# The pair loop's neighbour sums on TensorE moved one slot later, between two expert layers, and the output projection moved behind a first layer

## What is computed

```
xn  = layernorm(x)
gnn = segment_sum((xn @ W[rel])[src] * edge_weight, dst)        # 16 relations, 100,000 edges
mix = (attention(xn) * sigmoid(gelu(norm(xn) @ Wg1) @ Wg2)) @ Wproj + bproj
x   = x + gnn + mix
t   = layernorm(x)                                              # statistics of the new x
rw, re = top_2(softmax(t @ router.T)); combine = scatter(rw, re)
out = x + t + sum_e combine[:, e] * (gelu(t @ w1[e] + b1[e]) @ w2[e] + b2[e])
```

## Time and profile before

| | |
|---|---|
| median of 3 runs | 1621.45 us (1619.91 to 1625.02) |
| profiled execution | 1623.3 us, its span 1621.6 us |
| busy: TensorE, VectorE, ScalarE, GpSimd | 97%, 83%, 60%, 64% of the span |
| first phase | up to about 745 us |
| iterations 2 to 23 of the pair loop | 804 to 1544 us, 33.61 us each in the mean |

### The profile page before, as it was taken

How to read it: one execution, slowest core, us unless ns; L and a number is a source line. 1 busy time by engine, 2 the same in 40 slices (tenths; PEclk the granted TensorE clock), 3 DMA queues, 4 the chain that set the end, 5 groups by cost and what they waited for, 6 DMA issues and landing times.

```text
span 1621.6 us, 31747 instructions
## 1 busy us (share of the span) xinstructions
PE 1579.1 (97%) x10509; PEld 1442.6 (89%) x10509; DVE 1346.7 (83%) x3391; ACT 965.5 (60%) x2156; POOL 1030.0 (64%) x1109
## 2 busy tenths in 40 slices
PE   6899999999999999998699999999999999999998
PEld 5788888888888888887699999999999999999998
DVE  7878665488888888874699999999999999999985
ACT  4454222255655655553677766777667777677764
POOL 3443322577777777746777777777777777777720
PEclk9999999999999999999899999999999999999999
DMA  8677665688899888878433333343333333333320
GB/s 264 204 262 259 240 259 225 214 289 281 272 287 295 273 283 285 285 249 299 143 110 117 101 100 111 105 118 99 101 112 103 117 102 102 112 104 114 105 58 10
DMA packets 127076, 290.50 MB, mean 179 GB/s; under 512 B 21271, under 2 KB 49724, under 8 KB 126914
## 3 DMA queue, kind: packets, MB, share of 16 engines
q1 hardware_dynamic: 86068, 177.19, 29.8%
q0 software_dynamic: 39952, 110.13, 25.8%
q10 hardware_dynamic: 894, 1.16, 0.2%
HBM read 149.49 MB, written 138.90 MB: 178 GB/s over the span
## 4 chain that ended last, share of the span: by engine, by line
PE 68%; DVE 18%; issue 6%; ACT 3%; POOL 3%; DMA 1%; DVEq 0%; ACTq 0%; POOLq 0%
PE bank L1767 54%; DVE ml L1552 3%; DVE xres L1682 3%; DVE ht L1668 2%; POOL raw L685 2%; PE bank L1970 2%; PE bank L1811 2%; PE bank L1812 2%; DVE sel L1536 2%; PE bank L1971 2%; PE bank L1822 1%; PE bank L1922 1%; ACT mh L1010 1%; ACT raw L1066 1%; PE bank L1966 1%
## 5 line engine op out<-in xcount | busy, mean ns | idle before, releaser
L799 POOL DMA_INDIRECT stg<-table,idxcur x495 | 560.0, 1131 | 215.8 <-issue 114.7
L1767 PE MATMUL bank<-wreg,xt 128*128 128x512 f32 x2352 | 583.3, 399 | 4.9 <-DVE wreg L1151 2.3
L1767 PEld LDWEIGHTS bank<-wreg,xt 128*128 128x128 f32 x2352 | 436.6, 190 | 94.2 <-DVE wreg L1151 2.5
L685 POOL DMA_INDIRECT raw<-table,idxa x297 | 304.6, 1026 | 87.7 <-issue 75.6
L1767 PE MATMUL bank<-tt,wreg 128*128 128x256 f32 (+1 forms) x2400 | 318.6, 282 | 2.2 <-DVE tt L1618 2.2
L1767 PE MATMUL bank<-wreg,ht 128*128 128x256 f32 x2352 | 313.1, 282 | 0.2 <-DVE ht L1668 0.2
L1767 PEld LDWEIGHTS bank<-tt,wreg 128*128 128x128 f32 x2400 | 295.8, 189 | 5.4 <-issue 2.6
L1767 PEld LDWEIGHTS bank<-wreg,ht 128*128 128x128 f32 x2352 | 291.3, 188 | 0.4 <-DVE ht L1668 0.4
L1066 ACT ACTIVATE raw<-bank,cols 128x256 f32<-128x256 f32 (+1 forms) x400 | 165.0, 464 | 96.9 <-PE bank L1767 96.9
L1193 DVE COPY stg<-bank 128x512 f32<-128x512 f32 x196 | 133.6, 686 | 97.2 <-PE bank L1767 96.5
L1552 DVE SCALAR_TENSOR_TENSOR ml<-stg,nrm,mh 128x256 fp32r<-128x256 f32 x455 | 195.7, 480 | 16.0 <-ACT mh L1010 15.7
(11 more groups left out here) (244 smaller groups left out, 2136.8 us busy)
## 6 DMA issues: line engine op xcount, KB each, us to landing
table<-stg SPq DMA_DIRECT2D x196, 512.0 KB, 3.7
kv_d<-kvs SPq DMA_DIRECT2D x49, 256.5 KB, 5.2
xt_d<-xt SPq DMA_DIRECT2D x49, 256.0 KB, 4.6
xtp<-xt_d SPq DMA_DIRECT2D x24, 512.0 KB
stg<-table,idxcur POOLq DMA_INDIRECT x495, 2.9
sk<-kv_d SPq DMA_DIRECT2D x24, 256.5 KB, 5.7
out_x<-xres SPq DMA_DIRECT2D x24, 256.0 KB
xres<-in_x POOLq DMA_DIRECT2D x23, 256.0 KB, 4.5
```

The lines of the kernel that those rows point to most:

```text
L685: pool.indirect_dma_start(ring_a[:, r * EARLY + j, :], None, table[0:LIMIT, :], bass.IndirectOffsetOnAxis(ap=idxa[:, at:at + 1], axis=0)). ...
L799: pool.indirect_dma_start(stg[:, (s % 4) * SUP + j, :], None, table, bass.IndirectOffsetOnAxis(ap=idxcur[:, at:at + 1], axis=0)).then_inc( ...
L1767: mm = pe.matmul(dst, stat(a, c), mov(b, c), start=(n == 0), stop=(n == 3 * chunks - 1))
```

## The change

Only the order of steps changes, on TensorE alone (no other engine has a step called `SUMS` or `PROJ`). The sums of slot `s` are made in slot `s+1`, behind the slot's first expert layer and ahead of its second one, and the call names the slot of the sums (`*SUMS 0` in slot 1). In slot 6, `SUMS 5` comes last; slot 7 has `SUMS 6` behind `LAYER2 7` and its own sums at its end, as before. `PROJ` goes from the end of slot 2 to slot 3, between `LAYER1 5` and `SUMS 2`.

```diff
 SLOTS_OF_PAIR = (
-    ("-WEIGHT", "*SELECT", "-LOW 1", "*MSGS", "*WINDOW", "-COMB", "-COMB_HI", "-LAYER1 2", "-LAYER2 0", "*SUMS", "+OUT",
+    ("-WEIGHT", "*SELECT", "-LOW 1", "*MSGS", "*WINDOW", "-COMB", "-COMB_HI", "-LAYER1 2", "-LAYER2 0", "+OUT",
      "+GATES"),
-    ("-COMB_LOW", "*SELECT", "-ADD 0", "-LOW 2", "*MSGS", "+GATE_ACT", "+GATE", "-LAYER1 3", "-LAYER2 1", "+GATE_HI", "*SUMS"),
-    ("-ADD 1", "*SELECT", "-LOW 3", "*MSGS", "+GATE_LOW", "*WINDOW", "-LAYER1 4", "-LAYER2 2", "*SUMS", "+PROJ",
-     "-COMBT"),
-    ("-ADD 2", "*SELECT", "-LOW 4", "-COMBT_ACT", "*MSGS", "+STATS", "-LAYER1 5", "-LAYER2 3", "*SUMS"),
-    ("-ADD 3", "*SELECT", "-LOW 5", "*MSGS", "+MEAN", "*WINDOW", "-LAYER1 6", "+NORM", "-LAYER2 4", "*SUMS"),
-    ("-ADD 4", "*SELECT", "-LOW 6", "*MSGS", "*LAST_WINDOW", "-LAYER1 7", "+TURN", "+TURN_HI", "-LAYER2 5", "*SUMS",
-     "-BIAS2"),
+    ("-COMB_LOW", "*SELECT", "-ADD 0", "-LOW 2", "*MSGS", "+GATE_ACT", "+GATE", "-LAYER1 3", "*SUMS 0", "-LAYER2 1", "+GATE_HI"),
+    ("-ADD 1", "*SELECT", "-LOW 3", "*MSGS", "+GATE_LOW", "*WINDOW", "-LAYER1 4", "*SUMS 1", "-LAYER2 2", "-COMBT"),
+    ("-ADD 2", "*SELECT", "-LOW 4", "-COMBT_ACT", "*MSGS", "+STATS", "-LAYER1 5", "+PROJ", "*SUMS 2", "-LAYER2 3"),
+    ("-ADD 3", "*SELECT", "-LOW 5", "*MSGS", "+MEAN", "*WINDOW", "-LAYER1 6", "*SUMS 3", "+NORM", "-LAYER2 4"),
+    ("-ADD 4", "*SELECT", "-LOW 6", "*MSGS", "*LAST_WINDOW", "-LAYER1 7", "*SUMS 4", "+TURN", "+TURN_HI", "-LAYER2 5", "-BIAS2"),
     ("-ADD 5", "*SELECT", "+TURN_LOW", "-LOW 7", "*MSGS", "-BIAS2_ADD", "*WINDOW", "-LAYER2 6", "+LAYER1 0",
-     "+LOGIT", "*SUMS"),
-    ("-ADD 6", "*SELECT", "+LOW 0", "*MSGS", "+TOP", "-LAYER2 7", "+LAYER1 1", "-ADD 7", "*SUMS"),
+     "+LOGIT", "*SUMS 5"),
+    ("-ADD 6", "*SELECT", "+LOW 0", "*MSGS", "+TOP", "-LAYER2 7", "*SUMS 6", "+LAYER1 1", "-ADD 7", "*SUMS"),
 )
@@ in_slot @@
             if groups:
-                steps[name](i, s, groups)
+                steps[name](i, *map(int, expert or (s,)), groups)
```

## The result

Measured side by side, four executions each: 1665.47 us (1662.72 to 1668.82) against 1623.11 us (1619.91 to 1625.02) of the kernel before. The ratio is 1.0264, with a 95% interval from 1.0235 to 1.0293. The profiled execution of after has a span of 1660.9 us, 39.3 more than that of before. The forecast was 1655 us, with the range from 1636 to 1669.

What follows compares the result with a forecast made beforehand. TensorE was taken to set the pace, VectorE close behind; after the change, the loop through GpSimd's root. Pairs of 35.3 us against 33.69 added 35 over 22 iterations, +34 in all: 1657 profiled, 1655 us as median, range 1636 to 1669.

Steps and rivals of the forecast that it cites:

- The sign and the mechanism: Pair loop: slower, because later sums of slot 2 delay GpSimd's gathers and root, then `MEAN`, `TURN` and `LAYER1 0`; 70%.
- The sum: Whole kernel: 22 pairs at 1.6 us more give 35; with the other iterations, +34 us.
- Root to `MEAN`: GpSimd, second layer norm: time from the root's first instruction to `MEAN`, taken as 1.3 us (1.18 to 1.60).
- The rule that was weighed: VectorE and GpSimd share ports by exclusive lock: undisturbed root gives a 35.2 us pair, gathers and root hit give 35.9.
- Iteration 24: After the main pair loop: no gathers ahead of its root, so it only gains 0.9 us.
- The ramp: Iterations 0 and 1, waiting for gathers and weights: taken with the last two iterations at 0, plus or minus 4 us.
- `PROJ` a slot later: Slot 3: `PROJ` ends at 14.8 us, `STATS` asks for it at about 16.4; no cost.
- `WINDOW` in slot 6: VectorE waits about 0.8 us for sums 5; cost taken as 0, with 0.3 as the other end.
- `COMBT`: Comes earlier after the change, which frees ScalarE, off the path.
- The gain: Rival, pair loop: the root is not last, so 22 x 0.9 = 20 us come off, 1601 us; 10%.
- The half case: Rival: `LAYER1 0` not held by `TURN_LOW`, loss only at `TURN`, 0.8 us more a pair, 1639 us; 13%.
- The clock fell: Rival: TensorE's two waits a pair lower its clock, 27 us on top, 1682 us; 6%.

Runs made afterwards that it cites:

- run 10: The changed kernel with the root at (6, 2) and sums 5 ahead of `LAYER1 0`, on a chip like the first: 1618.95 us, ratio 0.9966 to the kernel before.
- run 9: The kernel before, unchanged, run again for its trace on a chip like the first: 1625.92 us in a single execution.
- run 11: The changed kernel with the root one gather earlier, ahead of the first gather of slot 7: 1640.84 us, ratio 1.0102 to the kernel before.
- run 3: The kernel before with only `PROJ` moved, behind `LAYER1 5` in slot 3: 1714.71 us, ratio 0.9982 to the kernel before.
- run 12: The changed kernel with `PROJ` back in slot 2, between `LAYER2 2` and `COMBT`: 1690.01 us, ratio 1.0414 to the kernel before.
- run 1: The changed kernel with the root moved from (7, 1) to (6, 2), two gathers fewer ahead of it: 1699.69 us, ratio 0.9899 to the kernel before.
- run 7: The kernel before with only the sums of slots 0 and 4 made a slot later: 1734.46 us, ratio 1.0092 to the kernel before.
- run 2: The changed kernel with the sums of slot 2 ahead of `PROJ` in slot 3: 1738.78 us, ratio 1.0124 to the kernel before.
- run 5: The changed kernel as it is, on the slower kind of chip: 1765.54 us, ratio 1.0252 to the kernel before.
- runs 1 to 8: The first eight follow-up runs, of variants of both kernels, on two chips where the kernel before takes 1718.6 and 1718.9 us.
- runs 3 and 4: The second of these: the changed kernel with sums 5 ahead of `LAYER1 0` in slot 6, 1713.36 us, ratio 0.9971 to the kernel before.

## Why the prediction was right

**The sign and the mechanism** were right. The view that gave it was GpSimd's order: nothing in the change touches GpSimd, and it is on GpSimd that the loss arises. Each step of the working, in us from the pair's start:

| step | forecast | measured (pair at 1301.41) |
|---|---|---|
| sums of slot 2 done | 15.56 | 15.43 |
| first gather of slot 6 | 16.35 | 16.22 |
| three gathers take | 4.0 (3.72 to 4.24) | 3.75 |
| root starts | 21.32 | 21.16 |
| root to `MEAN` | 1.3 (1.18 to 1.60) | 1.08 |
| `MEAN` | 22.6, waits 1.3 | 22.24, waits 1.14 |
| `MEAN` to `TURN` | 1.42 | 1.42 |
| `TURN` | 24.0, waits 1.8 | 23.66, waits 1.7 by starts |
| `MEAN` to `LAYER1 0` | 5.84, waits 0.8 | 5.79, waits 0.8 by starts |
| `LAYER1 0` to the next pair | 6.88 | 6.91 |
| pair | 35.3 (34.9 to 36.2) | 34.94; median 35.1, mean 35.20 |

**The sum.** 22 pairs gave 35.1 of the 35 forecast. That fits better than its terms do, and the last tenths are luck: the loop was set 0.2 to 0.4 us too long, 4 to 8 us in all, and two pairs at a lower clock (36.90 and 36.22 long, against 35.10) put 2.9 back. The pair that it was compared with, 33.69, was itself 0.09 longer than the mean of 33.60, which takes off another 2. What brought the median of the runs to 1665 instead of 1655 is therefore mostly outside the loop: the ramp's 3.8, iteration 24's 1.3, and the runs' median, which is 2.8 above the profiled execution's 1662.7 and had been taken 1.85 below it.

**Root to `MEAN`** was the one term outside its bounds: 1.08, where the nearest rows gave 1.18 and 1.60. In the pair at 1301 VectorE stood still from 1322.5 on, from just before the root's start until `MEAN`, and the root was quick. Both rows of the prediction stayed above that.

**The rule that was weighed.** The rows above have gathers of 0.95, 0.95 and 0.95, then one of 1.16, then the root in 1.08. The Trainium skill (SBUF — State Buffer, Who interferes with whom) states an exclusive lock on the ports that VectorE and GpSimd share. With a GpSimd left undisturbed by it in the root, the prediction came to 35.2. The trace lies on that side, at 34.94 and 35.1. But the rows do not show the lock as such: in the first three gathers VectorE was still at work, and none of them was slowed.

**Iteration 24** was mis-sized: said to gain 0.9, it lost 0.4. The root is no cause there (`TURN` has no bracket), but sums 5 stand behind `LAYER1 0` in it too, and TensorE waits for `TURN_LOW`, as its timeline in iteration 24 shows:

```profile
1605.08 0.66 PE L2008 MATMUL bank<-ident,scr 128*128 128x128 f32 x4
...
1609.44 1.67 PE L1767 MATMUL bank<-tt,wreg 128*128 128x256 f32 x12 [0.62 <-DVE tt L1618]
```

The step that failed is "has no gathers ahead of its root and only gains its 0.9": it followed one of two causes. With the second one taken away as well (run 10), iteration 24 does gain, 0.7.

**The ramp** was put at 0, plus or minus 4, and came to +3.8. Run 10 has the same 3.8 against its own before (run 9), but run 11, on the same chip, has 7.8, and the two traces of the kernel before differ by 2.9 at this point themselves (804.50 and 807.42, on two chips). So how much of it belongs to the change was not settled.

**What was said to cost nothing.** `PROJ` a slot later: right (run 3), and run 12 shows that it was needed. `WINDOW` in slot 6, taken at 0 with a wait of 0.8 us on VectorE: it waits 0.8 (15.7 us in 20), and in the table above nothing is left over for it. `COMBT`: no wait of it appears. One release was not listed at all: ScalarE's messages of slot S wait for the sums of S-2 as `SELECT` does (`act.wait_ge(edge_mm, S - 1)` in `MSGS`). In the waits of the profile after there is none before line 1010, so it cost nothing there (4.9 us in 14 in run 1).

**The rivals.** The gain did not come, because gathers and root take 6.8 us from sums 2 to `MEAN`; where that chain is shortened by two gathers, 2.5, and sums 5 fill the second hole (run 10), it does come, though 0.3% and not the 1.3% of 1601 us, since TensorE keeps 0.6 of the 1.0 that it saves. The half case fails at the point named: ScalarE's order does not change, and `LAYER1 0` is 5.8 behind `MEAN`. The clock fell, in 2 of 22 pairs.

**What stays open**: how much of run 7's loss is `TURN`, how much the messages and how much the chip; what an earlier release of the gathers is worth (run 2); what holds the engines on the slower chips; whether the loop over two pairs is what bounds the kernel of run 10; and whose the ramp's 3.8 us are.

## What to carry to other kernels

When a step moves on one engine, look at who is released by it and then at what stands behind that in the released engine's own order: here a two-instruction root stood behind four gathers, and the gathers alone did not mind being late. A wait at one place of a tight loop can be fixed by moving filler work to it; moving filler away from where it covers a long chain (here the sums of slot 5 from in front of `LAYER1 0`) opens a hole that no other wait explains. Count the work between an order and its use on the engine that will wait, before and after the move: it gave both holes here within 0.2 us.

## What the runs showed of the hardware

**The granted clock can fall behind a wait of 2.1 us.** In 2 of the 22 pairs (36.90 and 36.22 us long) the wait at `TURN` was 2.06 us, the longest of all. Busy time by stretch, kernel after (columns as above), and TensorE's timeline there:

```profile
1000.00:1005.00 5.00, 5.00 (x44) 5.00 (x44) 4.62 (x12) 3.17 (x7) 3.42 (x4) 1.00 0.54 179
1005.00:1010.00 5.00, 2.94 (x19) 2.74 (x18) 2.60 (x8) 2.82 (x7) 4.40 (x6) 0.83 0.29 82
1010.00:1015.00 5.00, 4.62 (x32) 4.41 (x31) 3.59 (x9) 3.08 (x8) 2.03 (x3) 0.83 0.27 79
1015.00:1020.00 5.00, 5.00 (x45) 5.00 (x44) 4.22 (x11) 2.31 (x5) 1.89 (x2) 1.00 0.08 25
```

```profile
1008.32 1.12 PE L2008 MATMUL bank<-ident,scr 128*128 128x128 f32 x4 [2.06 <-ACT scr L1031]
1009.09 2.85 PE L1767 MATMUL bank<-wreg,ht 128*128 128x256 f32 x12
```

TensorE had been full until the wait. Behind it the twelve matmuls of `LAYER2 5` take 2.85 us where they take 1.67 in the pair at 1301, and the granted clock of the two stretches is 0.83 in the mean, between its two levels of 1.2 and 2.4 GHz. In the pair at 1301, with 1.36 us of wait, the row behind `TURN` has its full speed. The pair is 36.90 long, 1.96 more than that one, with 0.7 more of wait: the lower clock adds some 1.3 us to a wait of 2.1. The other 20 waits in this trace were of 1.27 to 1.77 us, with no lower clock behind them. A wait of such a length does not always do it: in run 5, 12 of 17 waits of 2.1 to 2.6 us had a lower clock behind them and 5 had not.

**A second kind of chip.** On the chips of runs 1 to 8 the kernel before takes 1718.6 and 1718.9 us, 5.8% more than 1623.9. Iteration 2 begins at 861 to 876 us in their traces, against 804 to 815 on the first kind, and many pairs are longer by about 2 us (35.5 in run 3 beside 33.6 before). In those traces waits appear for which the profile names no engine of the core (`remote`, as GpSimd's 20.8 us in 11 in run 3); the traces on the first kind have none in the pair loop. What holds the engines there was not found. The sign of the comparison was the same on both kinds in the two cases that were measured on both (1.0264 and 1.0252; 0.9927 and 0.9966). The size was not for the second of them, and runs 3 and 4 show why: the two kernels of a comparison do not lose the same on the slower chips.
